# Decoder layer on one core: the last four groups' y turned to rows by transposing DMAs in 16-bit planes, and another order in the fold

## The reference

```
x = x + q * scan(sigmoid(a), kv)              # q, kv, a: thirds of rmsnorm(layernorm(x)) * gamma @ w_qkva
x = x + layernorm(softmax(q k^T) v @ Wout) * ln_scale + ln_bias
                                              # 16 heads of 64, 64 keys and a null key from ctx @ Wkv, q from layernorm(x) @ Wq
x = x + down(silu(gate(z)) * up(z))           # z = layernorm(x); weights ternary, activations 8 bits
```

## Time and profile before

| | |
|---|---|
| runs, us | 496.05, 493.4, 493.27; median 493.4 |
| profiled execution, us | 493.75 |
| its span, us | 492.0 |
| busy, us: PE, DVE, ACT, POOL | 461.9, 405.4, 328.8, 335.9 |
| DMA | 31.72 MB in 67129 packets |
| stage 1 / fold / step loop, us of the span | 0 to 98 / 98 to 157 / 157 to 492 |

### The profile page before, as it was taken

One profiled execution on the slowest core, in us unless ns is written; L12 is line 12 of the kernel. 1 busy time (PEld: TensorE's weight loads), 2 busy tenths in 40 slices (PEclk: granted clock), 3 DMA queues, 4 the chain that ended last, 5 costly groups with the idle time before them and its releaser, 6 DMA issues.

```text
span 492.0 us, 8077 instructions
## 1 busy us (share of the span) xinstructions
PE 461.9 (94%) x2580; PEld 362.7 (74%) x2580; DVE 405.4 (82%) x882; ACT 328.8 (67%) x429; POOL 335.9 (68%) x493
## 2 busy tenths in 40 slices
PE   1999999999999999999999999999999999999684
PEld 0777888777787788777778777878778777786432
DVE  4689987995566688998989989899898898997776
ACT  4456643144545344898888888889788888887552
POOL 2234455859752478897788787787877878888851
PEclk9999999999999999999999999999999999999979
DMA  8997000240000000012131121212322221212243
GB/s 264 325 369 279 3 1 1 42 87 1 1 1 1 0 1 6 12 29 59 37 55 40 37 60 40 54 38 48 51 43 50 43 54 41 52 39 59 48 106 99
DMA packets 67129, 31.72 MB, mean 64 GB/s; under 512 B 49680, under 2 KB 65296, under 8 KB 67088
## 3 DMA queue, kind: packets, MB, share of 16 engines
q1 hardware_dynamic: 67088, 31.21, 25.5%
HBM read 15.21 MB, written 4.19 MB: 39 GB/s over the span
## 4 chain that ended last, share of the span: by engine, by line
PE 77%; DVE 7%; POOL 6%; DMA 3%; ACT 3%; issue 2%; POOLq 0%; SPq 0%; ACTq 0%; DVEq 0%
PE psum L1346 31%; PE psum L1362 12%; PE psum L1636 10%; PE psum L1631 10%; PE psum L1608 3%; PE psum L1616 2%; PE psum L1445 2%; PE psum L1397 1%; PE psum L1497 1%; PE psum L1478 1%; PE psum L1381 1%; DMA gcol<-in_L_attn_gamma_dram 1%; DMA region_d<-region_d 1%; POOL xT1lo L555 1%; DVE region_a L1063 1%
## 5 line engine op out<-in xcount | busy, mean ns | idle before, releaser
L626 POOL TENSOR_TENSOR region_d<-region_d,rden 128x1024 f32<-128x1024 f32 x30 | 57.1, 1905 | 13.5 <-DVE rden L1148 13.1
L1631 PE MATMUL psum<-VW,region_d 128*128 128x256 f32 x256 | 60.7, 380 | 0.2
L1636 PE MATMUL psum<-VW,region_d 128*128 128x256 f32 x256 | 60.5, 379 | 0.0
L1128 DVE TENSOR_REDUCE mx<-psum 128x8 f32<-128x512 f32 x64 | 44.0, 688 | 14.3 <-PE psum L1346 13.1
L1346 PE MATMUL psum<-Mhi,xT2hi 128*128 128x512 f32 x128 | 53.6, 419 | 1.1 <-DVE xT2lo L1110 0.7
L1636 PEld LDWEIGHTS psum<-VW,region_d 128*128 128x128 f32 x256 | 48.6, 190 | 6.6
L1172 DVE SCALAR_TENSOR_TENSOR region_c<-psum,hzw,region_c 128x1024 f32<-128x1024 f32 x32 | 41.1, 1283 | 12.7 <-ACT region_c L845 12.5
L1631 PEld LDWEIGHTS psum<-VW,region_d 128*128 128x128 f32 x256 | 46.3, 190 | 6.4 <-ACT region_d L917 0.6
L1346 PE MATMUL psum<-Mhi,xT2lo 128*128 128x512 f32 x128 | 50.4, 393 | 0.0
L1346 PE MATMUL psum<-Mlo,xT2hi 128*128 128x512 f32 x128 | 50.1, 391 | 0.0
L562 POOL TENSOR_TENSOR pw_out<-pw_in,expo 128x8 f32<-128x8 f32 x8 | 13.2, 1648 | 44.1 <-DVE pw_in L1003 44.1
(11 more groups left out here) (165 smaller groups left out, 1203.1 us busy)
## 6 DMA issues: line engine op xcount, KB each, us to landing
out_dram<-xs SPq DMA_DIRECT2D x32, 128.0 KB, 1.9
xs<-in_x_dram SPq DMA_DIRECT2D x1, 2560.0 KB, 13.3
VW<-in_L_xattn_Wkv_dram SPq DMA_DIRECT2D x1, 2048.0 KB, 12.8
region_b<-in_L_xattn_Wkv_dram SPq DMA_DIRECT2D x1, 2048.0 KB, 16.9
xs<-in_x_dram SPq DMA_DIRECT2D x3, 512.0 KB, 7.2
region_w<-in_L_ffn_w_gate_dram SPq DMA_DIRECT2D x2, 512.0 KB, 10.1
region_w<-in_L_ffn_w_up_dram SPq DMA_DIRECT2D x2, 512.0 KB, 7.8
region_w<-in_L_ffn_w_down_dram SPq DMA_DIRECT2D x8, 128.0 KB, 5.2
```

The source lines that it names most:

```text
L626: pool.tensor_tensor(p_of(t).rearrange("p (h j) -> p h j", j=MK), e[:, :, 0:MK], rden[:, v, :].unsqueeze(2).broadcast_to([P, H, MK]), ALU. ...
L1128: dve.tensor_reduce(mx[:, hh, :], scores, AX.X, ALU.max).then_inc(max_done, 1)
L1631: pe.matmul(bank(7, D), pT[:, pair, :], VW[:, batch(n), pair, :], start=False, stop=False)
L1636: mm = pe.matmul(bank(7, D), pT[:, pair, :], VW[:, batch(n), pair, :], start=False, stop=pair == HC - 1)
```

## The change

For groups 4 to 7 (WHOLE_Y = 4) PE no longer transposes y. ACT splits y1, read as 16-bit halves, into two planes of 128x1024 (`y_planes`), two DMAs on SP's queue transpose one plane each, and ACT (for group 4 POOL) merges the turned planes into 32-bit rows (`merge_y`); POOL adds group 4 and DVE groups 5 to 7, from SBUF. The planes lie in the room of wv's first three quarters, which are therefore loaded only after x1(7). On PE, kv_T(0) stands ahead of the place of the last y's transposes, and the context's transposes stand ahead of the last q. POOL's context split comes ahead of rstd2(6), its splits 6 to 12 ahead of nvsel and Wout's additions. ACT normalises the second pair of tiles after the key loop; the order of its copies and exponentials and one place on DVE change. The first half of the first scores waits for half of Mlo. The diff, cut; blank lines are left out, and PE's `kv_T` and `stage1`, which changed places in the file, are shown by the lines that differ.

```diff
         yTs = f["kvT"].rearrange("p (t d) -> p t d", t=GT)
+        y_planes = f["wv"][:, 0:KD * GN].bitcast(I16).rearrange("p (s n) -> p s n", s=2)
+        y_planes_T = f["wv"][:, KD * GN:2 * KD * GN].bitcast(I16).rearrange("p (s j d) -> p s j d", s=2, d=P)
+        yTs_planes = f["wv"][:, 2 * KD * GN:3 * KD * GN]
         COPIED = 5
+        WHOLE_Y = 4
...
+        def y_plane(u, plane):
+            return a["y"][:, u * KD * GN:(u + 1) * KD * GN].bitcast(I16).rearrange("p (n s) -> p n s", s=2)[:, :, plane]
+        def merged_plane(plane):
+            return yTs_planes.bitcast(I16).rearrange("p (t k d s) -> p k t d s", t=GT, k=KD, s=2)[:, :, :, :, plane]
+        def turned_plane(plane):
+            return y_planes_T[:, plane, :, :].rearrange("p (k t) d -> p k t d", k=KD)
         def half(n):
             return n >> 1
...
-            sp.dma_start(wv, Wkv[:, INNER:2 * INNER].rearrange("(k p) n -> p k n", p=P)) \
-                .then_inc(wv_loaded, 16)
+            wv_rows = Wkv[:, INNER:2 * INNER].rearrange("(k p) n -> p k n", p=P)
+            sp.dma_start(wv[:, CC - 1:, :], wv_rows[:, CC - 1:, :]).then_inc(wv_loaded, 16)
...
+            def transpose_y(g):
+                for plane in range(2):
+                    sp.wait_ge(y_split, 2 * (g - WHOLE_Y) + plane + 1)
+                    if g > WHOLE_Y:
+                        sp.wait_ge(y_merged, 2 * (g - WHOLE_Y))
+                    sp.dma_start_transpose(y_planes_T[:, plane, :, :], y_planes[:, plane, :]) \
+                        .then_inc(y_plane_T[plane], 16)
+            for g in range(WHOLE_Y, NG - 1):
+                transpose_y(g)
             weight_T(0, wgT)
             weight_T(1, wuT)
+            transpose_y(NG - 1)
             weight_T(2, wdT)
+            sp.wait_ge(x1_done, NG)
+            sp.dma_start(wv[:, 0:CC - 1, :], wv_rows[:, 0:CC - 1, :]).then_inc(wv_loaded, 16)
             def transpose_h(t):
...
+                if g == NG:
+                    split_context()
                 if exists(g - 2, NG):
                     pool.wait_ge(ve2_done, g - 1)
                     pool.tensor_tensor(rstd2[:, (g - 2) * GT:(g - 1) * GT], ve2[:, :], expo[:, 0:GT], ALU.pow) \
                         .then_inc(rstd2_done, 1)
-                if exists(g - 1, COPIED):
+                if exists(g - 1, WHOLE_Y):
                     pool.wait_ge(yT_copied, g)
                     rows = xs[:, (g - 1) * GT:g * GT, :]
                     pool.tensor_tensor(rows, rows, yTs, ALU.add).then_inc(x1_done, 1)
+                elif exists(g - 1, COPIED):
+                    for plane in range(2):
+                        pool.wait_ge(y_plane_T[plane], 16)
+                        pool.tensor_copy(merged_plane(plane), turned_plane(plane)).then_inc(y_merged, 1)
+                    pool.wait_ge(y_merged, 2)
+                    rows = xs[:, (g - 1) * GT:g * GT, :]
+                    pool.tensor_tensor(rows, rows, yTs_planes.rearrange("p (t d) -> p t d", t=GT), ALU.add).then_inc(x1_done, 1)
                 if isinstance(g, int) and g == NG - 2:
                     pool.wait_ge(null_loaded, 64)
...
                     rounded(1)
                 if isinstance(g, int) and g == NG - 1:
                     rounded(2)
-                if g == NG:
-                    split_context()
             groups(stage1)
             split_kvw(WHOLE)
             split_kvw(WHOLE + 1)
+            for i in range(WHOLE + 2, HC + 5):
+                split_kvw(i)
             pool.wait_ge(nvsel_zero, 1)
             for row in (0, DH // 2):
                 pool.tensor_copy(nvsel[:, row:row + 1], nulls[:, 1:2]).then_inc(nv_set, 1)
             pool.wait_ge(wout_loaded, 16)
             pool.tensor_tensor(wsum, wout[:, 0, :], wout[:, 1, :], ALU.add).then_inc(wout_summed, 1)
             for pair in range(2, HC):
-                if pair > 3:
-                    split_kvw(pair + 2)
                 pool.wait_ge(wout_summed, pair - 1)
                 pool.tensor_tensor(wsum, wsum, wout[:, pair, :], ALU.add).then_inc(wout_summed, 1)
-            for i in range(HC + 2, HC + 6):
-                split_kvw(i)
+            split_kvw(HC + 5)
             def add_output(t):
...
+            def merge_y(g):
+                for plane in range(2):
+                    act.wait_ge(y_plane_T[plane], 16 * (g - WHOLE_Y + 1))
+                    if plane == 0:
+                        act.wait_ge(x1_done, g)
+                    act.activation(merged_plane(plane), turned_plane(plane), ACT.Copy).then_inc(y_merged, 1)
             def stage1(g, u):
                 v = 1 - u
-                if exists(g - 1, COPIED):
+                if exists(g - 1, NG) and g - 1 >= WHOLE_Y:
+                    act.wait_ge(y1_done, g)
+                    for plane in range(2):
+                        if g - 1 > WHOLE_Y:
+                            act.wait_ge(y_plane_T[plane], 16 * (g - 1 - WHOLE_Y))
+                        act.activation(y_planes[:, plane, :], y_plane(v, plane), ACT.Copy).then_inc(y_split, 1)
+                if exists(g - 1, WHOLE_Y):
                     act.wait_ge(yT_psum, g)
                     if positive(g - 1):
...
+                if g in (COPIED + 1, COPIED + 2):
+                    merge_y(g - 1)
                 if isinstance(g, int) and g == NG - 1:
...
                 put_kvT(i + 1)
                 if i == HC - 1:
                     xT2_pair(0, 0)
+                if i == 0:
+                    merge_y(NG - 1)
                 put_keys_hi(i)
                 if i == 5:
                     act.wait_ge(nmr2_done, NG)
                     norm2_pair(0, 0)
-                    norm2_pair(1, 1)
             def exponential(t):
                 act.wait_ge(shift_done, t + 1)
...
             put_kvT(HC + 1)
             put_kvT(HC + 2)
+            norm2_pair(1, 1)
             exponential(0)
+            put_values_second(0)
             put_kvT(HC + 3)
-            put_values_second(0)
             put_kvT(HC + 4)
             put_values_second(1)
+            put_kvT(HC + 5)
             exponential(1)
-            put_kvT(HC + 5)
             put_kvT(HC + 6)
             put_kvT(HC + 7)
+            put_values_second(2)
             xT2_pair(1, 1)
-            put_values_second(2)
             act.wait_ge(vnull_psum, 1)
             act.activation(vnull[:, :], psum[0:NR, 7, 0:D], ACT.Copy).then_inc(vnull_hi, 1)
...
+                if exists(g - 2, NG) and g - 2 >= COPIED:
+                    rows = xs[:, (g - 2) * GT:(g - 1) * GT, :]
+                    dve.wait_ge(y_merged, 2 * (g - 1 - WHOLE_Y))
+                    dve.tensor_tensor(rows, rows, yTs_planes.rearrange("p (t d) -> p t d", t=GT), ALU.add) \
+                        .then_inc(x1_done, 1)
                 if exists(g - 2, NG):
                     stats2(g - 2)
-                if exists(g - 1, NG) and g - 1 >= COPIED:
-                    rows = xs[:, (g - 1) * GT:g * GT, :]
-                    dve.wait_ge(yT_psum, g)
-                    dve.tensor_tensor(rows, rows, banks(6, 2).rearrange("p b (t d) -> p (b t) d", d=D), ALU.add) \
-                        .then_inc(x1_done, 1)
                 if exists(g + 2, NG):
...
-                    if positive(g - 1):
+                    if positive(g - 1) and g - 2 < WHOLE_Y:
                         dve.wait_ge(yT_psum, g - 1)
+                    elif positive(g - 1):
+                        dve.wait_ge(y_split, 2 * (g - 1 - WHOLE_Y))
                     dve.tensor_tensor(y1[:, u, :, :], banks(2, 2), hid[:, u, :, :], ALU.mult) \
                         .then_inc(y1_done, 1)
...
                 softmax_half(t, 1, t)
+                if t == 0:
+                    put_values_first(0)
                 exp_sum(t, t)
                 exp_sum_reciprocal(t, t)
                 if t == 0:
-                    put_values_first(0)
                     put_values_first(1)
             put_values_first(2)
...
+                if g == NG:
+                    kv_T(0)
+                if exists(g - 1, WHOLE_Y):
+                    pe.wait_ge(y1_done, g)
+                    if positive(g - 1):
...
+                if isinstance(g, int) and g == NG - 1:
+                    pe.wait_ge(ctx_loaded, 16)
+                    pe.wait_ge(xT1_ready, NG)
+                    for k in range(CC):
...
                 mm.then_inc(xT2_psum, 1)
-            kv_T(0)
             pe.wait_ge(wq_loaded, 16)
             pe.wait_ge(y1_done, NG)
             wq_T(0)
...
                 kv_T(i + 2)
                 fold_keys(i)
                 if i == HC - 2:
-                    pe.wait_ge(x1_done, NG)
+                    pe.wait_ge(wscale_done, 2)
                     pair_T(0, 0)
             def scores_half(n, hh, u4, q, b):
...
                     .then_inc(sim_psum, 1)
             kv_T(HC + 2)
-            pe.wait_ge(m_lo, 2 * HC)
             for hh in range(2):
+                pe.wait_ge(m_lo, (hh + 1) * HC)
                 scores_half(0, hh, 0, 0, 0)
```

55 lines of the change are left out of this document (27 added, 28 removed).

## The result

| | before | after |
| --- | --- | --- |
| median of 11 runs each | 493.40 us | 490.51 us |
| lowest and highest | 492.01 to 496.05 | 488.87 to 492.51 |
| the profiled execution, span | 493.75, 492.0 | 492.51, 490.7 |
| its mean granted clock | 0.991 | 0.984 |

The ratio is 0.9937, with a 95% interval of 0.992 to 0.9955: 2.9 us less, which is within 1%. 491.5 was predicted, with 489.4 to 494.6. The profiled execution of after is the slowest of its eleven; the single executions of a kernel spread by 1.8 to 5.2 us here (0.4 in e_swap, which has four), and their mean granted clocks lie between 0.979 and 0.999. So medians say what a change is worth, and the traces say where, by differences of moments inside one trace.

What follows compares the result with a forecast made beforehand. After 97.5 us DVE's queue and the port, not PE, were taken to set kv_T(4). +0.9 there, -1.45 and -1.35 in the fold make -1.9 us: 491.5 for the median, range 489.4 to 494.6.

Steps and rivals of the forecast that it cites:

- PE's four blocks gone: Stage 1: four blocks of y transposes leave PE, kv_T(0) starts 4.1 us earlier, all eaten before kv_T(4).
- What bounded kv_T(4): End of stage 1: DVE's queue and the port put kv_T(4) at 111.9, 0.9 us later than before.
- POOL served first: At DVE and POOL's holds: add(6) waits for both context split halves, wqT1 ends at 107.5, kv_T(4) starts at 112.4.
- DVE first: At the same holds: ternary(2) waits for the context split, wqT1 is done at 105.9, kv_T(4) starts at 110.8.
- the free rival: Before kv_T(4): larger additions not held, add(7) waits for planes to 105.6, kv_T(4) at 110.25; 489.9 us, chance 0.17.
- The port: SBUF shared by DVE and POOL: of two contending instructions, the one that issues second blocks fully, larger additions included.
- case L: Stage 1 on DVE: add(5) held behind rounded(1), kv_T(4) 1.75 us later; 493.7 or 492.1 us, chance 0.25.
- The fold's first part, 1.45: From kv_T(4) to the first scores: PE's waits of 0.62, 0.22, 0.22 and 0.39 us go, 1.45 in sum.
- The second part, 1.35: Fold from the scores on: fold_values(1) 0.6 earlier, kvT(13) 0.4, put_values_second(2) 0.2, other waits about 0.15; sum 1.35.
- ACT's and POOL's planes: Stage 1: splits and merges take 1.05 to 1.1 us each; hidden on ACT but the last four, group 4's on POOL hidden.
- The late load: 1.5 MB of wv behind x1(7), hidden with 10.9 us of room; as slower rival 493.3 to 497.5, chance 0.06.
- The clock: PE, no size given: the prediction is wrong if PE's granted clock falls behind its idle time.

Runs made afterwards that it cites:

- e_swap: The changed kernel with group 7's two planes ahead of wuT's transpose on SP's queue, nothing else; 487.21 us, ratio 0.9867 to before.
- e_planes: The changed kernel with the fold's five pieces back in their old order, so the planes alone; 493.45 us, ratio 0.9983 to before.
- e_fold: The kernel before with only the fold's five pieces in their new order, y still on PE; 490.35 us, ratio 0.9936.

## Why the prediction was right, and where it was not

- **PE's four blocks gone, and nothing gained by it.** Right: from y1(4) to kv_T(4) the table has +0.99 us, the sum had +0.9; e_planes, the same code up to there, has +0.55, so that the tenth is chance.
- **What bounded kv_T(4).** The number was right by two errors that cancel. Since the execution began 1.19 us sooner than that of before, its moments stand beside the predicted ones with 1.19 added. y1(7) ends at 96.9 (97.1 predicted), wqT1 at 104.85: not at 107.5, as with POOL served first, to which I had leaned, and 1.05 before even the 105.9 of DVE first, outside the 106 to 107.5 that were to show the mechanism. But group 7's merges end at 107.0 and not at 105.9, because the planes are issued 0.5 later behind wuT and a merge takes 0.3 more than I took. So the bound of this stretch was the planes, for 2.15 us, and not DVE's queue and the port; kv_T(4) came at 112.0 where I had 111.9. I had a wait for the planes in the free rival alone, and did not ask what their place behind wuT cost; e_swap shows 2.2 us.
- **The port.** The small operation L1037 took 0.99 at 97.03 beside POOL's cast, and POOL's subtraction lost 0.94 when DVE's addition stood first. The trace agrees with the rule named in the prediction (the Trainium skill, "SBUF — State Buffer", Who interferes with whom): whoever issues second is held. At the two hand-overs at which both had one waiting DVE went first: L1069 at 86.93 and POOL's pass at 87.08, L1069 at 97.94 and the subtraction at 98.08. So L1069 was never held (three times, mean 1216 ns; at the third POOL stood idle). The forecast had leaned to POOL first there. The first of the two also decided against case L, by 0.15 us.
- **The fold's first part, 1.45.** The places were right, the size was short: e_fold shows 2.08. The terms were the idle times in the brackets. Measured from start to start against the same step without a wait, the four waits of before cost 0.70, 0.33, 0.47 and 0.55, which is 2.05, since the matmuls behind a stop are slower too (the group at 131.49 takes 0.50 for its first matmul, others 0.40).
- **The second part, 1.35.** 1.25 in after, 1.21 in e_fold: right.
- **ACT's and POOL's planes.** The splits took 1050 ns, as said. The merges took 1369 on ACT and 1360 on POOL and not 1.05, so the merge, which reads in another order and writes with a stride, costs 0.3 more than the split; both were hidden but the last. The transposes took 1.3 us each to issue (median), the first behind wuT 1.7, and 3.4 to landing; 1.24 and 3.1 were predicted.
- **The late load.** 1.5 MB landed in 6.4 us, room was 10.9: hidden, as said.
- **The clock.** It stood among the things that would make it wrong, with no price. It cost 2.2 us in the profiled execution. The median was nevertheless 1.0 below the prediction, inside its own range. Of that 0.6 is the fold. A lower clock can only add time, and with the measured terms and none of it the sum is 0.99 - 2.08 - 1.25 = -2.3, where the medians have -2.9: at least 0.6 us of the gain has no term in it. e_planes shows the same gap, +0.61 from y1(4) to p in the trace and 0.24 less than before by the medians. What it is stays open, and that the forecast came so near is partly luck.
- **The bound from below.** PE's 4.1 and the fold's 2.8 in full would give 486.5, not the 488.5 for which the prediction wanted them both. e_swap reached 487.2 with 4.6 us in its trace (1.2 at kv_T(4), 3.4 behind it).
